# An attention stage re-ordered by sequence: single-sequence steps, a shared FFN spread over four of them, and the state products in other PSUM banks

## What is computed

```python
x = x + xattn(layernorm(x), ctx, ctx, ...)   # 16 x 256 x 256, 8 heads
#   ig, fg = gates of [q, k, v];  cs = cumsum(log_sigmoid(fg))
#   log_D = tril(cs_s - cs_t + ig_t);  D = exp(log_D - max log_D)
#   C = (q k^T / sqrt(32)) * D
#   h = C / (max(|sum C|, exp(-max log_D)) + EPS) @ v, then a layer norm over the features
x = x + ffn(layernorm(x), ...)
#   logits = x @ gate_w.T; softmax; top 32 columns for each of 16 experts (gather, expert FFN, scatter-add)
#   shared = (gelu(x @ Ws_g.T) * (x @ Ws_u.T)) @ Ws_d.T      # width 512
x = x + xattn2(layernorm(x), ctx)
x = x + ffn2(layernorm(x), ...)              # top 2 of 8 experts, width 1024
```

## Time and profile before

| | before |
|---|---|
| three runs | 1460.94, 1471.44, 1470.69 us (median 1470.69) |
| profiled execution | 1463.27 us, with a span of 1461.4 us |
| PE busy in the span | 1204.6 us (82%) |
| DVE busy | 998.9 us (68%) |
| ACT busy | 792.1 us (54%) |
| POOL busy | 703.9 us (48%) |
| mean granted TensorE clock | 0.874 of full speed |
| stage 1 (first instruction to last store) | 0 to 454.4 us |

### The profile page before, as it was taken

How to read it: one execution, slowest core, us unless ns; L and a number is a source line. 1 busy time by engine, 2 the same in 40 slices (tenths; PEclk the granted TensorE clock), 3 DMA queues, 4 the chain that set the end, 5 groups by cost and what they waited for, 6 DMA issues and landing times.

```text
span 1461.4 us, 24552 instructions
## 1 busy us (share of the span) xinstructions
PE 1204.6 (82%) x8542; PEld 1113.5 (76%) x8542; DVE 998.9 (68%) x2012; ACT 792.1 (54%) x1541; POOL 703.9 (48%) x634
## 2 busy tenths in 40 slices
PE   3588887978984999999967772499999999999930
PEld 2567776867873888888856662499999999999930
DVE  4477676567533666665625663399999999999958
ACT  3345553454131665565526441477777777777724
POOL 2223343133224466566441567255555565556548
PEclk9557897878897999999987875699999999999975
DMA  5533142231003676666537983233333333333247
GB/s 169 183 131 130 56 138 84 102 109 51 15 31 129 182 190 190 188 181 175 133 45 250 277 219 73 49 56 56 56 56 55 56 56 56 56 59 56 48 112 251
DMA packets 144555, 164.67 MB, mean 113 GB/s; under 512 B 30577, under 2 KB 124913, under 8 KB 142385
## 3 DMA queue, kind: packets, MB, share of 16 engines
q1 hardware_dynamic: 114016, 124.98, 27.6%
q0 software_dynamic: 29312, 37.31, 15.2%
q10 hardware_dynamic: 1104, 0.82, 0.2%
HBM read 118.28 MB, written 44.78 MB: 112 GB/s over the span
## 4 chain that ended last, share of the span: by engine, by line
PE 66%; DVE 9%; issue 5%; POOL 4%; DMA 3%; ACT 2%; another core or an unknown queue 1%; POOLq 1%; SPq 0%; ACTq 0%; DVEq 0%
PE quad L1812 15%; PE pb L1831 15%; PE quad L1129 11%; PE pb L1144 5%; PE pb L370 5%; PE pb L384 4%; PE quad L309 3%; PE pb L355 2%; POOL dSL L1692 2%; DMA c3T<-in_ctxT 1%; PE quad L1793 1%; PE pb L1114 1%; PE quad L298 1%; POOL dACC L1270 1%
## 5 line engine op out<-in xcount | busy, mean ns | idle before, releaser
L1876 DVE TENSOR_TENSOR wl<-W,wh 128x1024 fp32r<-128x1024 f32 x156 | 188.8, 1231 | 51.0 <-ACT gl L1945 26.0
L1983 POOL DMA_INDIRECT dOUT<-y,es x78 | 127.0, 1628 | 187.1 <-DVE y L1901 175.2
L1919 ACT CAST wh<-W 128x1024 fp32r x117 | 122.8, 1050 | 114.8 <-PE pb L1831 90.7
L1831 PE MATMUL pb<-wh,hh 128*128 128x256 f32 x624 | 179.9, 288 | 1.1 <-DVE hl L1893 0.8
L1831 PE MATMUL pb<-wh,hl 128*128 128x256 f32 x624 | 176.4, 283 | 0.0
L1831 PE MATMUL pb<-wl,hh 128*128 128x256 f32 x624 | 176.4, 283 | 0.0
L1893 DVE TENSOR_TENSOR hl<-gl,hh 128x512 fp32r<-128x512 f32 x156 | 162.6, 1063 | 8.8 <-ACT hh L1950 4.2
L1270 POOL DMA_INDIRECT dACC<-ye,idxJ x64 | 100.8, 1576 | 103.4 <-ACT ye L1233 54.3
L1945 ACT ACTIVATE gl<-quad,b1c 128x256 f32<-128x256 f32 x312 | 130.3, 469 | 15.4 <-PE quad L1812 9.6
L1812 PE MATMUL quad<-xh,wh 128*128 128x256 f32 x624 | 126.6, 285 | 1.5 <-issue 1.5
L1812 PE MATMUL quad<-xl,wh 128*128 128x256 f32 x624 | 126.4, 284 | 0.0
(11 more groups left out here) (271 smaller groups left out, 3351.7 us busy)
## 6 DMA issues: line engine op xcount, KB each, us to landing
MB<-dM SPq DMA_DIRECT2D x16, 1024.0 KB, 5.0
W<-in_W SPq DMA_DIRECT2D x16, 1024.0 KB
wraw<-in_Wg SPq DMA_DIRECT2D x16, 512.0 KB
wraw<-in_Wu SPq DMA_DIRECT2D x16, 512.0 KB
wraw<-in_Wd SPq DMA_DIRECT2D x16, 512.0 KB
b2c<-in_b SPq DMA_DIRECT2D x39, 128.0 KB
xp<-in_x SPq DMA_DIRECT2D x16, 256.0 KB, 5.7
cT<-in_ctxT SPq DMA_DIRECT2D x16, 256.0 KB, 5.4
```

What stands on the lines that cost most here:

```text
L1831: ins = pe.matmul(bank.t[:, 0:256], a_[s][:, c, 128 * tt:128 * tt + 128], b_[n % 3][:, 256 * c:256 * c + 256], start=half == 0 and m == 0, ...
L1876: v.tensor_tensor(w_dst(wl[n % 3], kind), w_src(expert(i), kind, half), w_dst(wh[n % 3], kind), ALU.subtract).then_inc(*v_t.up("w", n))
L1919: a.copy(w_dst(wh[n % 3], kind), w_src(expert(i), kind, half)).then_inc(*a_t.up("w", n))
L1983: g.indirect_dma_start(out=dOUT[:, :], out_offset=bass.IndirectOffsetOnAxis(ap=es[i % 6][:, tt, 1:2].bitcast(U32), axis=0), in_=y1[i % 2][ ...
```

## The change

The thirteen cycles become 27 steps, `STEPS1 = range(-7, 20)`, one for each sequence: step s has the attention of sequence x = s, the tail of y = s-1, the router of z = s-2, and the preparation of q = s+7. Two steps take the place of a cycle. The pieces of the shared FFN are spread over four steps: pair p has `up(p, 0, 0)` at the end of step 2p+2, `up(p, 0, 1)`, `up(p, 1, 0)`, `up(p, 1, 1)` in step 2p+3, slices 2 and 3 in step 2p+4, and `down` in step 2p+5. `up` is now called for each half m, `values` for each half c, `weigh_scores` for each half c. The state products leave the `misc` banks and go into quad banks 2 and 3, over the scores, so `state` now stands behind `values(x, 0)`, which waits until all scores have been read. ACT, DVE, POOL and SP programs are rewritten in the same steps. The last pair still ends in the last two steps, as before.

```diff
-        CYCLES = range(-3, 10)
+        STEPS1 = range(-7, 20)
...
-            def values(b):
-                for c in range(2):
-                    for k in range(2):
-                        if c == 0:
-                            pe.wait_ge(*v_att.of("C", b, 1, 1))
...
+            def values(b, c):
+                if c == 0:
+                    pe.wait_ge(*v_att.of("C", b, 1, 1))
+                    pe.wait_ge(*a_att.of("V", b))
+                for h in range(NH):
+                    ins = pe.matmul(quad[:, c, 33 * h:33 * h + 33], Dm[b % 2][:, c, h, :], V[b % 2][:, c, h, :], start=True, stop=True)
+                ins.then_inc(*pe_att.up("CV", b, c))
...
             def state(b):
-                bank, was = misc.take(("KV", b), v_att, "KV", b)
-                if was:
-                    pe.wait_ge(*was)
                 pe.wait_ge(*g_att.of("wV", b))
                 for k in range(2):
-                    ins = pe.matmul(bank[:, 132 * k:132 * k + 132], cb[b % 2][:, 0, 128 * k:128 * k + 128],
+                    ins = pe.matmul(quad[:, 2, 132 * k:132 * k + 132], cb[b % 2][:, 0, 128 * k:128 * k + 128],
                                     wV[b % 2][:, 4 * k:4 * k + 4, :], start=True, stop=True)
...
+            for s in STEPS1:
+                x, y, z, q = seq(s), seq(s - 1), seq(s - 2), seq(s + 7)
+                p, p1 = pair_of(s // 2 - 2), pair_of(s // 2 - 1)
+                if x is not None:
+                    scores(x)
+                if s % 2 == 0:
+                    if p is not None:
+                        up(p, 2, 0)
+                    if z is not None:
+                        router(z)
+                    if p is not None:
+                        up(p, 2, 1)
+                    if x is not None:
+                        values(x, 0)
+                    if p is not None:
+                        up(p, 3, 0)
+                    if x is not None:
+                        state(x)
+                    if y is not None:
+                        h_transposed(y)
+                    if x is not None:
+                        values(x, 1)
+                    if p is not None:
+                        up(p, 3, 1)
+                    if q is not None:
+                        q_transposed(q)
+                    if x is not None:
+                        from_state(x)
...
+                    if p1 is not None:
+                        up(p1, 0, 0)
+                    if s % 4 == 0 and 0 <= s // 4 + 1 < 4:
+                        gates(s // 4 + 1)
+                else:
+                    if p is not None:
+                        down(p, 0)
+                    if z is not None and z != 15:
+                        router(z)
+                    if p is not None:
+                        down(p, 1)
+                    if x is not None:
+                        values(x, 0)
+                    if p is not None:
+                        down(p, 2)
+                    if x is not None:
+                        state(x)
+                        values(x, 1)
+                    if p is not None:
+                        down(p, 3)
+                    if x is not None:
+                        from_state(x)
+                    if p1 is not None:
+                        up(p1, 0, 1)
+                    if y is not None:
+                        h_transposed(y)
+                    if p1 is not None:
+                        up(p1, 1, 0)
...
+                    if p1 is not None:
+                        up(p1, 1, 1)
```

```diff
+                if xn is not None:
+                    decay(xn, 0)
+                if s % 2 == 0:
+                    if p is not None:
+                        gelu(p, 2)
+                    if z is not None:
+                        logits(z)
...
+                    if p is not None:
+                        h_round(p, 2)
+                    if x is not None:
+                        o_copy(x)
+                    if p is not None:
+                        gelu(p, 3)
+                    if y is not None:
+                        h_copy(y)
...
+                if s % 2 == 0:
+                    if x is not None:
+                        weigh_scores(x, 0)
+                        weigh_scores(x, 1)
...
+                    if y is not None:
+                        tail_residual(y)
+                    if p is not None:
+                        gate_up(p, 2)
...
+                    if qn is not None:
+                        norm_x(qn)
+                    if y is not None:
+                        tail_norm(y)
+                    if x is not None:
+                        mask_state(x)
+                    if q is not None:
+                        norm_q(q)
+                    if y is not None:
+                        split_h(y)
```

More of the change, by code:

```diff
@@ L220, in build, with seq, pair_of @@
         misc = in_turn(banks[6:8])
[L221 to L239 removed]
+        STEPS1 = range(-7, 20)
+        def seq(b):
+            return b if 0 <= b < B else None
+        def pair_of(p):
+            return p if 0 <= p < B // 2 else None
         def heads(b):
@@ L322, in from_state @@
             def from_state(b):
-                bank, was = misc.take(("qKV", b), v_att, "O", b)
-                if was:
-                    pe.wait_ge(*was)
                 pe.wait_ge(*v_att.of("KV", b))
                 for k in range(2):
-                    ins = pe.matmul(bank[:, 132 * k:132 * k + 132], qT[b % 8][:, k, 128:256], KV[b % 2][:, k, :, :], start=True, stop=True)
+                    ins = pe.matmul(quad[:, 3, 132 * k:132 * k + 132], qT[b % 8][:, k, 128:256], KV[b % 2][:, k, :, :], start=True, stop=True)
                 ins.then_inc(*pe_att.up("qKV", b))
@@ L357, in router, with up @@
                 ins.then_inc(*pe_tail.up("lg", b))
[L359 to L373 removed]
+            def up(p, f, m):
+                if p or f:
+                    pe.wait_ge(*(a_ffn.of("gelu", *prev(p, f)) if m == 0 else v_ffn.of("gf", *prev(p, f))))
+                if f == 0 and m == 0:
+                    pe.wait_ge(*v_tail.of(2 * p + 1, "Hl"))
+                    if p == 0:
+                        pe.wait_ge(*v_w.of("ws", 2))
+                n = 0
+                for w, x in ((wsh, Hh), (wsh, Hl), (wsl, Hh)):
+                    for k in range(2):
+                        ins = pe.matmul(banks[4 + m].t[:, :], w[:, m, 512 * k + 128 * f:512 * k + 128 * f + 128],
+                                        x[p % 2][:, k, :], start=n == 0, stop=n == 5)
+                        n += 1
+                ins.then_inc(*pe_ffn.up("up", p, f, m))
             def down(p, tt):
@@ new lines, in gate_weights, with other_weights @@
+            def gate_weights():
+                v.wait_ge(*small_ld.all())
+                v.wait_ge(*const_g.of("gb0"))
+                v.tensor_copy(gw[:, :, 0:2, 0:8], gw0[:, :, 0:2, :])
+                v.tensor_tensor(gw[:, :, 2:4, 0:8], gw0[:, :, 2:4, :], gw0[:, :, 4:6, :], ALU.add).then_inc(*v_w.up("gates"))
+            def other_weights():
+                v.wait_ge(*rw_ld.all())
+                v.tensor_copy(rth[:, :, :], rw[:, :, :]).then_inc(*v_w.up("rth"))
+                v.wait_ge(*v_w.of("rth"))
+                v.tensor_tensor(rtl[:, :, :], rw[:, :, :], rth[:, :, :], ALU.subtract).then_inc(*v_w.up("router"))
+                for m in range(3):
+                    v.wait_ge(*a_w.of("ws", m))
+                    v.tensor_tensor(wsl[:, m, :], ws_raw(m), wsh[:, m, :], ALU.subtract).then_inc(*v_w.up("ws", m))
@@ L1043, in sp_stage1 @@
             sp.dma_start(rw[:, :, :], A["gate_w"].rearrange("(k p) e -> p k e", p=128)).then_inc(*rw_ld.up("rw", by=16))
-            for c in CYCLES:
-                bs, nx, g, p = pair(c), pair(c + 1), group_of(c), ffn(c)
-                if c == -3:
-                    for b in (2, 3):
+            for s in STEPS1:
+                y, p = seq(s - 1), pair_of(s // 2 - 2)
+                g = (s + 3) // 4 if s % 4 == 1 and 0 <= (s + 3) // 4 < 4 else None
+                if s == -7:
+                    for b in range(2, 5):
                         ctxT_in(b)
@@ L1074, in sp_stage1 @@
                         sp.dma_start(dACC[r0:r0 + 128, :], ys[tt % 2][:, :]).then_inc(*acc_st[tt % 2].up(p, tt, by=16))
-                if bs:
-                    h_out(bs[1])
             for s in (*acc_st, *H_st):
```

465 lines of the change are left out of this document (193 added, 272 removed).

## The result

The changed kernel took 1491.9 us (median of 4 runs) against 1465.8 us for the kernel before on the same chip: the ratio is 1.0172, with a 95% interval from 1.0104 to 1.024. The forecast of 1439 us is missed by more than its range allowed. Slow executions are left out of the ratios: one each of e1 (1501.6 us), e10 (3997) and e12 (2838), and one of the kernel before (1524.8).

A forecast was written before the change was run, and what follows sets the result against it. The prediction took PE as the bound, not at full speed (mean clock 0.84). From 1463.3 us it took 17 for the steady part and 7 for the end, with zero for the start: 1439 us, range 1415 to 1468.

The forecast's parts named there:

- The even step's waits: Even steps: DVE waits about 2 us each for ACT and POOL, PE's `h_transposed` waits for `tail_norm`; `tail_heads` ends at 19.5.
- its clock term: Even-step pieces behind `tail_norm`: 4.7 us at full speed, 9 at half; about half the loss taken, six times 2.5 = 15.
- the odd step: Walk from DVE's last instruction of the step before, at full clock: `split_h` 14.4, `tail_heads` 17.7, `gate_up` of slice 1 18.4 us.
- the 20 us on top: Steady part: 20 us added to six times 37.9 = 227.5 for `gates`, `forget_1`, `forget_2` and the first routing, giving 247.
- I cost it at nothing: SP's `max_in` behind the four `down` stores in odd steps: no cost; without its lead up to 5.0 us a pair.
- `tail_heads`: DVE operation in both step walks, sized at 3.3 us from the kernel before.
- I take zero, from -6 to +7: Start: decays used by halves, up to 6 us earlier, against `gates(1)` ahead of `scores(1)`, twice 3.6 us; zero taken.
- The table loads: ACT in even steps: two loads of 1.28 us, so four a pair instead of two; the change's own cost.
- The end: From the last `values` to the last store: about 43 us instead of 50.4, a gain of 7.
- Rival D: Slower by the clock: short waits hold it at 0.75, 51.3 us a pair, 1485 us in all; chance 0.13.
- Rival C: Steady part: clock stays at 0.84, a pair takes 46.5 us as now, only the end gains: 1456 us; chance 0.27.
- The forecast gain of 17 us in the steady part: Steady part, `scores` of sequence 4 to step 16: 262 us instead of 279, from 247 plus 15 for the clock.

The follow-up runs named there:

- e1: The changed kernel with four `ys` tiles in place of two: ratio 1.0153 to the kernel before.
- e10: e6 with two `ys` tiles again: ratio 1.0011 to the kernel before.
- e12: e6 plus six unread matmuls in even steps between `values(x, 1)` and `h_transposed(y)`: 1446.2 us, ratio 0.9899 to the kernel before.
- e6: The changed kernel with four `ys` tiles, `norm_x(4)` behind `norm_q(3)`, even-step decays late, `h_transposed` behind `values(x, 1)`: 1457.6 us, ratio 0.9939 to the kernel before.
- e2: The changed kernel with `norm_x(4)` put behind `norm_q(3)` at the start: ratio 1.0231 to the kernel before.
- e14: e6 with the first half decay of even steps back ahead of `gelu(p, 2)`: ratio 1.0001 to the kernel before.
- e3: The changed kernel with the first half of even steps' decays moved to the end of the step: ratio 1.0191 to the kernel before.
- e9: The changed kernel itself measured once more, on the third chip: ratio 1.0235 to the kernel before.
- e8: The kernel before with unread matmuls, eight ahead of `q_transposed` of the second sequence and fourteen ahead of `down(p, 0)`: ratio 0.9934 to the kernel before.
- e15: e12 with `state(x)` of odd steps ahead of `down(p, 2)`: ratio 0.9895 to the kernel before.
- e11: e6 with `state(x)` of odd steps ahead of `down(p, 2)`: ratio 0.9948 to the kernel before.

## Why the prediction was wrong, step by step

**The even step's waits and its clock term were right.** Every wait that was named came, at the named place and near the named size (ACT 1.66 us for "about 2", POOL 2.08 for "about 2"). "I take about half, six times 2.5 = 15" held too: from the start of `h_transposed` to the end of `from_state` the six even steps took 6.3, 7.5, 8.8, 7.9, 6.9 and 7.9 us where the walk has 4.7 at full speed, 2.9 more on average. That the half was a choice between two bounds, and not read from a row, makes this partly luck.

**The step that failed is the odd step, "`split_h` 14.4, `tail_heads` 17.7, `gate_up` of slice 1 18.4", walked at full clock and without a wait for a store.** Taken from the starts of `scores`, the six even steps average 25.4 us and the six odd ones 25.0, where the forecast comes to 19.5 + 2.5 + 1.7 = 23.7 and 18.4 + 1.7 = 20.1 (1.7 being a twelfth of the 20 us on top). So 6 x 4.9 = 29 us of the 40 lie in odd steps, with the 20 us spread evenly; more of them belong to steps 5 and 9 with the `forget` operations, and none of the others comes down to 20.1 either. No clock term stood there at all, yet PE's busy time in odd steps holds 17 us more than its full-speed work (30 in even steps). And DVE waited 24.6 us for stores. The two overlap, and no run prices the clock of the odd steps by itself.

**"I cost it at nothing" failed by omission.** The sentence was about `max_in` behind the four stores. The waits of `causal` for MB that did come, 16.1 us in steps 5 and 9, are for loads issued ahead of those stores; they were on the prediction's list of what would make it wrong, and their price is open. The same queue read the other way round was a cost: the stores stand behind `h_out(y)`, which waits for `tail_norm`, and `add_down(p, 2)` waits for a store. The prediction asked what SP's new order does to `max_in`, but not which engine waits for each of the transfers that were moved. By e10 this is worth 0.7% of the time, about 10 us.

**`tail_heads` was mis-sized.** Its 3.3 us are of the kernel before. In the changed kernel it took 4.5 to 5.2 us in the six even steps and 3.4 to 3.9 in the odd ones, some 12 us in all, and both walks run through it. The first two operations are slow. In step 6 they run beside the split of hhs and `causal` on POOL, where the kernel before has POOL idle (L538 is L535 before):

```profile
209.61 1.10 POOL L985 TENSOR_SCALAR_AFFINE_SELECT MB<-MB 128x1024 f32<-128x1024 f32 x1
209.73 1.00 DVE L538 SCALAR_TENSOR_TENSOR nn<-nn,cols 128x16 f32<-128x16 f32 x1
```

```profile
235.44 0.18 DVE L535 SCALAR_TENSOR_TENSOR nn<-nn,cols 128x16 f32<-128x16 f32 x1
```

No edit moves `causal` away from `tail_heads`, and e6 has the same lengths, so what this costs in time is not shown.

**"I take zero, from -6 to +7" for the start.** It came out at +5.9 us, inside the bounds, but by a mechanism that was not named: not `gates(1)` on PE, but the order of `norm_x(4)` and `norm_q(3)` on DVE, whose load comes late. With that order mended (e2) sequence 4 starts at 120.9 us, 4.0 earlier than before. The chain to the first `scores` was not walked like the steady steps, and so the 10.2 us at that point weren't seen.

**The table loads.** The stretch has 28 table loads after (25 of them at the decays' and the gelu's lines, 1.28 us each) where it had 13. The Trainium skill ("ScalarE: Activation LUTs", Table sets) advises batching by table set. In e14 against e6, 28 loads against 16, ACT is busy 19.5 us more and the time is 0.6% longer, but in e3 against the changed kernel the same 12 loads fewer brought nothing that shows above the uncertainty. So the advice agrees with the rows once the other waits are gone, as far as one edit can tell that takes loads away and moves the decays at once. In the even step's walk the loads stood where they came, at their size.

**The end was right**: 44.4 us for "about 43". **Rival D had the direction**: "slower at all below a mean clock of 0.82", and the clock was 0.81 (0.76 in e9). Its 1485 us is the profiled execution's 1484.6, but by chance: D had all of the loss in the clock at 0.75 with 6 us of idle time a pair, while the trace has 0.81 and 7.8. With the clock at 0.81 and 6 us of idle time D's own sum gives only 2 us more than before; the rest is idle time and the late start. It was given little weight because the walk's pieces were added up as if every hand-over but the named ones were free; the same text said under C that small hand-overs come to 4%.

**Rival C describes the mended kernel.** e6 has no store wait, no early loads and no swapped groups, and its steps still need the old kernel's time at the old clock of 0.84. C gave 1456; e6 took 1457.6 beside 1465.2 of the kernel before, a gain of 7.6 us where C's was 7. The forecast gain of 17 us in the steady part wasn't there even without the mistakes of the order; only with the clock at 0.89 (e12) does the stretch come out shorter, by 5.9 us. The Trainium skill ("TensorE: Matmul & The Clock Gate", Why this matters for your kernels) wants no long idle gaps on PE; e8 and e12, in which such gaps are filled, agree with it, at 0.84 to 0.93 and 0.84 to 0.89.

## What to carry to other kernels

When an order is rewritten, list for each transfer that is moved in an in-order queue not only what it waits for but who waits for it to finish, above all a ring's next writer: here a store behind a wait of another tensor stopped DVE for 7.9 us. Put work that is ready between a producer on another engine and the PE group that needs it; a swap of two groups was worth 1.3%. And when several causes are suspected, mend them together and then leave out one at a time, with enough executions for the size that is looked for: three of the four showed nothing clear alone, where other waits stood behind them and the uncertainty was as large as their 0.5 to 0.7%.

## What the runs showed of the hardware

Matmuls whose results are never read made the kernel before faster, and most likely the mended one too. In e8, 22 in a cycle raised the mean clock of the stretch from 0.84 to 0.93 and took 0.66% [0.34, 0.98] off the time. In e12, six in every even step are the only difference to e6 and raise it from 0.84 to 0.89; e15 and e11 differ in the same way (0.9895 [0.9863, 0.9928] and 0.9948 [0.9926, 0.997]). A pause of 2.5 us on PE, after a step with 33-column groups in it, was followed by 6 us at 1.2 GHz with PE busy all through (198 to 208 us of the changed kernel). The mean clock of one program is not fixed: the same stretch of the changed kernel ran at 0.81 in one execution and at 0.76 in another, 7 us apart. A DVE operation on 16 elements a partition with two inputs (`tail_heads`) took 1.00 us while POOL ran `causal`, 0.54 beside a shorter POOL operation (231.0 us of the changed kernel), and 0.18 with POOL idle (235.4 us of the kernel before).
